# The last stage of a four-layer graph network on Trainium2: thirteen units of four node columns instead of whole-tile steps

## The reference, cut to what matters

```
out  = segment_sum(xl[src] * softmax(logits by dst), dst) + bias     # [N, 4 heads * 16]
mean = out.mean(axis=0); var = out.var(axis=0)                       # over the 6,250 nodes
out  = (out - mean) * rsqrt(var + 1e-5) * gamma + beta
y    = x + gelu(out + x)
result = (y - y.mean(-1)) / sqrt(y.var(-1) + 1e-5)                   # over the 64 features
```

## Time and profile before

| what | us |
|---|---|
| median of 3 runs | 6778.48 (6776.0 to 6781.07) |
| the profiled execution's own time | 6777.28 |
| its span | 6775.5 |
| start of the first gather of the last stage | 6614.07 |
| start of VectorE's work behind the gathers | 6679.11 |
| start of the first store | 6767.56 |

### The profile page before, as it was taken

How to read it: one execution, slowest core, us unless ns; L and a number is a source line. 1 busy time by engine, 2 the same in 40 slices (tenths; PEclk the granted TensorE clock), 3 DMA queues, 4 the chain that set the end, 5 groups by cost and what they waited for, 6 DMA issues and landing times. The chain is left out here.

```text
span 6775.5 us, 58450 instructions
## 1 busy us (share of the span) xinstructions
PE 3900.6 (58%) x12498; PEld 2265.4 (33%) x12498; DVE 3850.9 (57%) x4586; ACT 1823.0 (27%) x3467; POOL 3542.2 (52%) x3649
## 2 busy tenths in 40 slices
PE   3556544675444444444444435777778787777770
PEld 2344432454222222222222223333344344433340
DVE  9988844632333333333333343777787778777774
ACT  1233322342111111111111111333333333333330
POOL 5430032215666666666666656665666556565542
PEclk7666667765776676666676655666666656666665
DMA  5545577502343334333343312333333333333320
GB/s 157 166 155 165 163 164 197 181 8 59 95 102 100 102 99 103 98 102 98 101 103 98 100 40 58 81 84 75 82 86 84 80 80 86 80 81 78 81 69 22
DMA packets 1365705, 671.25 MB, mean 99 GB/s; under 512 B 1042970, under 2 KB 1246324, under 8 KB 1364706
## 3 DMA queue, kind: packets, MB, share of 16 engines
q1 hardware_dynamic: 1090118, 338.26, 21.0%
q0 software_dynamic: 116096, 120.71, 9.5%
q10 hardware_dynamic: 159390, 211.24, 8.9%
HBM read 344.19 MB, written 325.64 MB: 99 GB/s over the span
## 5 line engine op out<-in xcount | busy, mean ns | idle before, releaser
L1565 POOL DMA_INDIRECT got<-tabg,ix x1568 | 1479.0, 943 | 960.3 <-issue 426.0
L1373 POOL DMA_INDIRECT got<-tabg,ix x1568 | 1479.0, 943 | 830.8 <-issue 441.9
L1393 PE MATMUL p_inter<-hid,W 128*128 128x512 f32 x392 | 381.1, 1073 | 1251.9 <-DVE run L1479 983.9
L1471 DVE TENSOR_TENSOR_SCAN own<-mk,own,p_first 128x512 f32<-128x512 bf16 x195 | 248.8, 1276 | 1419.3 <-remote 806.0
L175 PEld LDWEIGHTS p_out<-ident,run 128*128 128x128 f32 (+1 forms) x3136 | 580.8, 219 | 577.7 <-issue 572.1
L175 PE MATMUL p_out<-ident,run 128*128 128x128 f32 (+1 forms) x3136 | 684.2, 372 | 64.5 <-issue 57.0
L490 DVE TENSOR_TENSOR_SCAN run<-p_mk,run,feat 128x512 f32<-128x512 f32 x390 | 477.2, 1265 | 243.2 <-ACT feat L583 84.1
L1393 PEld LDWEIGHTS p_inter<-hid,W 128*128 128x128 f32 x392 | 93.6, 297 | 1295.9 <-issue 1163.3
L1728 DVE TENSOR_TENSOR p_pre<-own,p_pre 128x512 f32<-128x512 f32 x196 | 136.0, 694 | 561.0 <-issue 313.5
L1617 PE MATMUL p_logit<-act_in,AT 128*128 128x512 f32 x392 | 288.7, 826 | 284.9 <-DVE act_in L1734 157.2
L558 PE MATMUL p_mk<-mk,sel 2*128 2x512 bf16 x392 | 166.5, 517 | 450.8 <-DVE run L490 367.3
(11 more groups left out here) (309 smaller groups left out, 7414.7 us busy)
## 6 DMA issues: line engine op xcount, KB each, us to landing
t<-rows ACTq DMA_DIRECT2D x195, 512.0 KB
first<-start SPq DMA_DIRECT2D x780, 128.0 KB
t<-rows ACTq DMA_DIRECT2D x195, 288.0 KB
got<-tabg,ix POOLq DMA_INDIRECT x3136
start<-zeros SPq DMA_DIRECT2D x100, 500.0 KB
ea<-in_ea_dram SPq DMA_DIRECT2D x390, 128.0 KB
mk<-marks SPq DMA_DIRECT2D x780, 64.0 KB
start<-zeros SPq DMA_DIRECT2D x195, 256.0 KB
```

Source lines behind the costliest of these rows:

```text
L1373: nc.gpsimd.indirect_dma_start(got[s][0:g.p, cc, h, :], None, tabg, bass.IndirectOffsetOnAxis(ap=ix[0:g.p, g.n, h, cc:cc + 1], axis=0)).th ...
L1393: nc.tensor.matmul(p_inter[s][:, 0:g.w], W2[:, :], hid[s][:, 0:g.w], start=True, stop=True).then_inc(mixed, 1)
L1471: nc.vector.tensor_tensor_scan(own[s][:, 0:g.w], mk[m][:, 0:g.w], p_first[s][:, 0:g.w], prime[:, 0:1] if g.zero else own[1 - s][:, W - 1:W ...
L1565: nc.gpsimd.indirect_dma_start(got[s][0:g.p, cc, h, :], None, tabg, bass.IndirectOffsetOnAxis(ap=ix[0:g.p, g.n, h, cc:cc + 1], axis=0)).th ...
```

## The change

`finish_4` becomes one block, and `norm` goes. Everything but the clearing, two small preparations and `X + BE` runs by the 13 units of `UNITS`:

- Each unit has its own semaphore for its four gathers. VectorE makes the differences of a unit (`shift`), ScalarE the exponentials (both in one instruction), VectorE the messages (`attend`, one unit behind).
- The sums over nodes are 49 accumulating matmuls each, one for each node column, with `ones` as weights, or `some` (ones only on the full partitions) from column 27 on. For the variance ScalarE squares a unit and TensorE sums it.
- Scale, gelu, residual sum and the last norm's mean and squares run by units in one loop; the last root is still one for all nodes.
- The final scaling goes by units, and SyncE stores each unit behind it. `out_rows` yields the 127 full partitions as one transfer, and in units that reach below column 27 a second one for the last partition: 13 + 7 = 20 transfers.

```diff
@@ -816,42 +816,6 @@
-def norm(nc, sb, sem, ahead, t, o, behind):
...
+def out_rows(out, a, k):
+    yield slice(0, FULLP), k, out[0:FULLP * NJ, :].rearrange("(p j) f -> p j f", j=NJ)[:, a:a + k, :]
+    last = min(LASTJ - a, k)
+    if last > 0:
+        yield slice(FULLP, FULLP + 1), last, out[FULLP * NJ + a:FULLP * NJ + a + last, :].rearrange("(p j) f -> p j f", p=1)
...
             def _(sp):
...
+                stores = 0
+                for u, (a, k) in enumerate(UNITS):
+                    sp.wait_ge(done, u + 1)
+                    for part_, j, rows_out in out_rows(out, a, k):
+                        sp.dma_start(rows_out, out_y[part_, a:a + j, :]).then_inc(written, 16)
+                        stores += 1
+                sp.wait_ge(written, 16 * stores)
             @block.gpsimd
             def _(pool):
                 pool.wait_ge(cleared, 1)
-                gather_rows(pool, nc, rows, T3, t3, info["last"], rows_in)
+                for u, (a, k) in enumerate(UNITS):
+                    for j in range(a, a + k):
+                        nc.gpsimd.indirect_dma_start(rows[:, j, :], None, t3, bass.IndirectOffsetOnAxis(ap=info["last"][:, j:j + 1], axis=0),
+                                                     bounds_check=E - 1, oob_is_err=False).then_inc(rows_in[u], 16)
...
+                def shift(u):
+                    a, k = UNITS[u]
+                    dve.wait_ge(rows_in[u], 16 * k)
+                    wait_from(dve, raised, u - 1)
+                    wait_from(dve, shifted, 2 * u)
+                    link(nc.vector.tensor_tensor(mx[:, 0:k, :], theirs[:, a:a + k, :], rows[:, a:a + k, D + HEADS:T3], ALU.max))
+                    nc.vector.tensor_tensor(dif[u % 2][:, 0:k, 0, :], rows[:, a:a + k, D + HEADS:T3], mx[:, 0:k, :], ALU.subtract).then_inc(shifted, 1)
+                    nc.vector.tensor_tensor(dif[u % 2][:, 0:k, 1, :], theirs[:, a:a + k, :], mx[:, 0:k, :], ALU.subtract).then_inc(shifted, 1)
+                def attend(u):
+                    a, k = UNITS[u]
+                    f, q = fac[u % 2], part[u % 2]
+                    dve.wait_ge(raised, u + 1)
+                    mark(nc.vector.tensor_tensor(q[:, 0:k, 0, :], rows[:, a:a + k, D:D + HEADS], f[:, 0:k, 0, :], ALU.mult))
+                    link(nc.vector.tensor_tensor(q[:, 0:k, 1, :], f[:, 0:k, 1, :], heads(carry[:, D:D + HEADS], k), ALU.mult))
+                    link(nc.vector.scalar_tensor_tensor(out=denom[:, 0:k, :], in0=q[:, 0:k, 0, :], scalar=1e-16, in1=q[:, 0:k, 1, :], op0=ALU.add, op1=ALU.add))
+                    link(nc.vector.reciprocal(rden[:, 0:k, :], denom[:, 0:k, :]))
+                    mark(nc.vector.tensor_tensor(q[:, 0:k, 0, :], f[:, 0:k, 0, :], rden[:, 0:k, :], ALU.mult))
+                    link(nc.vector.tensor_tensor(q[:, 0:k, 1, :], f[:, 0:k, 1, :], rden[:, 0:k, :], ALU.mult))
+                    mark(nc.vector.tensor_tensor(split(msg[:, 0, 0:k, :]), split(rows[:, a:a + k, 0:D]), channels(q[:, 0:k, 0, :], k), ALU.mult))
+                    link(nc.vector.tensor_tensor(split(msg[:, 1, 0:k, :]), split(each(carry[:, 0:D], k)), channels(q[:, 0:k, 1, :], k), ALU.mult))
+                    link(nc.vector.tensor_tensor(msg[:, 0, 0:k, :], msg[:, 0, 0:k, :], msg[:, 1, 0:k, :], ALU.add))
+                    nc.vector.tensor_tensor(Y[:, a:a + k, :], msg[:, 0, 0:k, :], each(BI, k), ALU.add).then_inc(ys, 1)
+                def centre(u):
+                    a, k = UNITS[u]
+                    nc.vector.tensor_tensor(Y[:, a:a + k, :], Y[:, a:a + k, :], each(mean, k), ALU.subtract).then_inc(centred, 1)
+                def scale(u):
+                    a, k = UNITS[u]
+                    link(nc.vector.tensor_tensor(Y[:, a:a + k, :], Y[:, a:a + k, :], each(rg, k), ALU.mult))
+                    nc.vector.tensor_tensor(Y[:, a:a + k, :], Y[:, a:a + k, :], XB[:, a:a + k, :], ALU.add).then_inc(zs, 1)
+                def centre_2(u):
+                    a, k = UNITS[u]
+                    dve.wait_ge(gelus, u + 1)
+                    link(nc.vector.tensor_tensor(out_y[:, a:a + k, :], Y[:, a:a + k, :], X[:, a:a + k, :], ALU.add))
+                    link(nc.vector.tensor_reduce(s_sum[:, a:a + k], out_y[:, a:a + k, :], AX.X, ALU.add))
+                    link(nc.vector.tensor_scalar(s_mean[:, a:a + k], s_sum[:, a:a + k], 1.0 / D, None, ALU.mult))
+                    nc.vector.tensor_tensor(out_y[:, a:a + k, :], out_y[:, a:a + k, :], bn(s_mean[:, a:a + k], k), ALU.subtract).then_inc(zc, 1)
+                def spread_2(u):
+                    a, k = UNITS[u]
+                    dve.wait_ge(z2, u + 1)
+                    nc.vector.tensor_reduce(s_var[:, a:a + k], sq[u % 2][:, 0:k, :], AX.X, ALU.add).then_inc(v2, 1)
...
+                link(nc.vector.tensor_copy(some[:, :], valid[:, LASTJ:LASTJ + 1].to_broadcast((P, P))))
+                mark(nc.vector.tensor_scalar(away[:, :], info["span"][:, :], -1.0, -NEG, ALU.add, ALU.mult))
...
+                nc.vector.tensor_tensor(XB[:, :, :], X[:, :, :], per_feature(BE), ALU.add).then_inc(ready, 1)
+                for u in range(NU + 1):
+                    if u < NU:
+                        shift(u)
+                    if u:
+                        attend(u - 1)
+                dve.wait_ge(total, NU)
+                link(nc.vector.tensor_scalar(mean[:, :], p_sum[:, :], 1.0 / N, None, ALU.mult))
+                for u in range(NU):
+                    centre(u)
+                dve.wait_ge(ready, 1)
+                dve.wait_ge(centred, NU)
+                link(nc.vector.tensor_tensor(rg[:, :], rs[:, :], GA[:, :], ALU.mult))
+                for t in range(NU + 4):
+                    if t < NU:
+                        scale(t)
+                    if 0 <= t - 2 < NU:
+                        centre_2(t - 2)
+                    if 0 <= t - 4 < NU:
+                        spread_2(t - 4)
+                dve.wait_ge(root, 1)
+                dve.wait_ge(zc, NU)
+                link(nc.vector.reciprocal(s_rs[:, :], s_sd[:, :]))
+                for a, k in UNITS:
+                    nc.vector.tensor_tensor(out_y[:, a:a + k, :], out_y[:, a:a + k, :], bn(s_rs[:, a:a + k], k), ALU.mult).then_inc(done, 1)
...
+                def nodes(j):
+                    return some if j >= LASTJ else ones
+                pe.wait_ge(chain, 3)
+                for u, (a, k) in enumerate(UNITS):
+                    pe.wait_ge(ys, u + 1)
+                    for j in range(a, a + k):
+                        mm = nc.tensor.matmul(p_sum[:, :], nodes(j)[:, :], Y[:, j, :], start=j == 0, stop=j == NJ - 1)
+                    mm.then_inc(total, 1)
+                for u, (a, k) in enumerate(UNITS):
+                    pe.wait_ge(squared, u + 1)
+                    for j in range(a, a + k):
+                        mm = nc.tensor.matmul(p_var[:, :], nodes(j)[:, :], sq[u % 2][:, j - a, :], start=j == 0, stop=j == NJ - 1)
+                    mm.then_inc(spread, 1)
             def _(act):
+                for u, (a, k) in enumerate(UNITS):
+                    act.wait_ge(shifted, 2 * u + 2)
+                    wait_from(act, ys, u - 1)
+                    nc.scalar.activation(fac[u % 2][:, 0:k, :, :], dif[u % 2][:, 0:k, :, :], ACT.Exp).then_inc(raised, 1)
+                for u, (a, k) in enumerate(UNITS):
+                    act.wait_ge(centred, u + 1)
+                    wait_from(act, spread, u - 1)
+                    nc.scalar.activation(sq[u % 2][:, 0:k, :], Y[:, a:a + k, :], ACT.Square).then_inc(squared, 1)
+                act.wait_ge(spread, NU)
+                nc.scalar.activation(sd[:, :], p_var[:, :], ACT.Sqrt, scale=1.0 / N, bias=eps[:, 0:1]).then_inc(rooted, 1)
+                for t in range(NU + 3):
+                    if t < NU:
+                        a, k = UNITS[t]
+                        act.wait_ge(zs, t + 1)
+                        nc.scalar.activation(Y[:, a:a + k, :], Y[:, a:a + k, :], ACT.Gelu).then_inc(gelus, 1)
+                    if 0 <= t - 3 < NU:
+                        u, (a, k) = t - 3, UNITS[t - 3]
+                        act.wait_ge(zc, u + 1)
+                        wait_from(act, v2, u - 1)
+                        nc.scalar.activation(sq[u % 2][:, 0:k, :], out_y[:, a:a + k, :], ACT.Square, scale=0.125).then_inc(z2, 1)
+                act.wait_ge(v2, NU)
+                nc.scalar.activation(s_sd[:, :], s_var[:, :], ACT.Sqrt, bias=eps[:, 0:1]).then_inc(root, 1)
...
-        norm(nc, sb, sem, [], Z, Y, [])
...
```

More of the change, by code:

```diff
@@ L1763, in finish_4 @@
         carry = sb(c, "carry", [P, T3])
-        Y, Z = sb(c, "Y", [P, NJ, D]), sb(c, "Z", [P, NJ, D])
+        Y, XB, out_y = sb(c, "Y", [P, NJ, D]), sb(c, "XB", [P, NJ, D]), sb(c, "out_y", [P, NJ, D])
         BI, GA, BE = (sb(c, n, [P, D]) for n in ("BI", "GA", "BE"))
-        inv = sb(c, "inv", [P, NJ])
-        theirs, mx, dif, fac, scaled, denom, rden = (sb(c, n, [P, NJ, HEADS]) for n in ("theirs", "mx", "dif", "fac", "scaled", "denom", "rden"))
```

(35 more changed lines are left out.)

93 lines of the change are left out of this document (5 added, 88 removed).

## The result

The changed kernel takes 6864.07 us in the median (6823.18 to 6881.47, 4 runs), the kernel before 6779.77 in the same session (6776.0 to 6792.22): a ratio of 1.0108, 95% interval 1.0078 to 1.0138. Slower, as forecast (the interval lies clear of 1), but 39 us above the forecast of 6825 and outside its range of 6803 to 6847. That is a coincidence, which a table of the stages brings out. Each number is the distance between two instructions of the timeline: the first memset of the last stage, its first gather, the mean, the reciprocals `rs` and `s_rs`, the end of the span.

A forecast was written before the change was run, and what follows sets the result against it. It took the last stage as bound by GpSimd's gathers (65 us), then VectorE (88), then stores and barrier (9). −25.8 + 5.0 + 1.1 + 0.6 + 66.3 = +47.2 on 6777.28 led to 6825, range 6803 to 6847.

The forecast's parts named there:

- Messages by units, beside the gathers: Last stage's message loop: 3.0 us a unit hides behind 5.2 for its four gathers, so centring starts 25.8 us earlier.
- the rival of slower gathers: Last stage's gathers: VectorE's load slows them by up to 12 us, giving 6837; chance 0.03.
- My own sign: VectorE's last reciprocal, forecast near 6744: if later than 6750, the steps before the stores were mispriced.
- Variance, +5.0: Centring to reciprocal of the root: 49 TensorE matmuls 0.43 us apart make it 22.5 us instead of 17.46, 5.0 lost.
- The rival of a rising clock: Variance: TensorE at full clock, so 49 matmuls take 13.5 us instead of 21.1, giving 6817; chance 0.08.
- Scale, gelu, last norm, +1.1 and +0.6: Loop after the variance: 32.7 us against 31.6, 1.1 lost; last root waits for its table load, 0.6 lost.
- Stores, +66.3: Final stores of 127 partitions queue on one engine: 78.6 us from reciprocal to end instead of 12.3, 66.3 lost.
- The other end of my range: Store stream on one engine at 26 GB/s, 62 us, giving 6812; packet price well off to either side, chance 0.12.
- the divisor rule: Stores: a transfer uses as many engines as the largest divisor of its partitions up to 16, so 127 get one.
- The closing packets: Final stores: small packets that close a transfer on each engine, forecast as 20 instead of 32.
- The sum: Whole change: −25.8 + 5.0 + 1.1 + 0.6 + 66.3 = +47.2 us on the profiled execution's 6777.28.

The follow-up runs named there:

- the large units: Messages of the last stage over four units of 12, 12, 12 and 13 columns instead of 13 units; in the kernel with all repairs, ratio 0.9968 and 0.9969.
- the repaired ones: The changed kernel with stores cut at 112 in three groups, 256-column matmuls for node sums, sum of x and beta behind centring: ratio 0.9958 and 0.9953.

## Why the prediction was wrong

**The failed step is "Messages by units, beside the gathers": centring "25.8 us earlier", "hidden" behind GpSimd.** It gained 3.2 us in the first session, 22.6 less than forecast. The sum put the lateness of hand-offs beside the gathers at nothing. The instructions were sized right: 3.05 us a unit against 3.0 (the loop that waits for all rows). Two things failed. The larger one, some 19 us, is that on that chip hand-offs beside a long run of gathers come 0.4 to 4.5 us late (up to 5.2 in the later traces with lateness), and a unit has seven in a row on VectorE, and one to ScalarE and back. On chip 4, without lateness, the same kernel gains 22.0. Where the lateness comes from stays open. I looked for a slowdown of the gathers by VectorE, and not for one of VectorE by the gathers. My evidence that "VectorE runs beside many of those scatters" came from the earlier trace rows, the durations of GpSimd's instructions; the waits of the other engines in the same chains, shown above, were in the same trace. The smaller one, 3.3 us, is the second gather beside the sum of x and beta: the rival of slower gathers was right in kind, for one gather only, and with a 3.42 us instruction as its cause.

My own sign came true: `s_rs` ended at 6751.35, later than 6750, though the stage had begun 15.5 us early.

**Variance, +5.0:** measured +5.0, paced by TensorE at half clock as said. The rival of a rising clock did not come with 64 columns; it came with 256.

**Scale, gelu, last norm, +1.1 and +0.6:** measured +1.9 together. The table load stands ahead of the last root as said.

**Stores, +66.3:** mechanism right, shown by 54 us on taking it out and on putting it in; size 8.5 us too large. The stream ran at a flat 24 GB/s where I took 22.1 from a transfer that had all 16 engines at work; 1.60 MB at 24 is 67 us, not 75, and 4 were left for lead and tail. The other end of my range, 26 GB/s from the fastest slice, was as near in rate and nearer in time (62 us). By the divisor rule ("DMA: Bandwidth & Descriptors", section "Why a DMA increments its semaphore by 16 and not by 1", of the Trainium skill) 127, 124 and 112 partitions give 1, 4 and 16 engines, and the traces agree: 6.8% and 21.2% of 16 engines, and 54 us between the first and the last. The closing packets are 20, as forecast: the queue shows 1678 packets from 6750 to 6822, of which 1658 are data by my count (12 × 127 + 127 + 7).

**The sum:** +47.2 forecast, +61.5 measured in the first session (22.6 from the messages, less 8.5 from the stores, 0.2 from the loop), +42.8 on chip 4 (3.8 from the messages, less 8.4, the rest alike). There the ratio is 1.0063 (1.0043 to 1.0083); +47.2 on that chip's 6099.4 would be 1.0077, inside that interval. Between the stage's +61.5 and the medians' +84 lie 23 us. They were traced nowhere; I take it that they arose in stages that the change leaves alone, since the two sets have four runs each, of which one spans 58 us, and since the difference of medians was 60 us, the stage's 59, when the changed kernel ran eight times against 27 runs of the one before. The stage's miss of 14 us alone would have left the time inside my range, at 6839; with the 23 it fell outside. That the profiled execution lay 1.7 us from the forecast was luck. My range allowed for nothing of that kind; the 5 us between runs of before in the listed times were no guide to it.

## What to carry to other kernels

Before cutting a store by columns, look at its partitions: 127 ran on one engine at 24 GB/s and 124 on four, and a few wide pieces of 112 with small ones beside them cost less than any of these. Before hiding a chain of short dependent steps beside a run of gathers, find chains in the trace that already run beside one and read the idle time ahead of their instructions, not the instructions' durations: where they stand until the gathers end, the overlap brings less than half of what it does elsewhere (14.8 us on chip 9 against 32 between chips 0 and 4). And compare stages before totals, for a total that fits can be two errors.

## What the runs showed of the hardware

- Sessions, each on its own chip, differ in how soon signals arrive. On the three with late ones the kernel before took 6764 to 6855 us, on the three without 6097 to 6111 (medians, or one execution on chips 13 and 0). The stages between differ too: from the memset that opens layer 2's edges to the second node chain it is 2337 us (first session) and 1979 (chip 4), from there to the last stage 2653 and 2508. In the view of waits (total, count, longest) the longest wait of one weight load that the profile can't explain falls from 18.3 us (first session) to 3.7 (chip 4):

```profile
PEld p_inter L1393 <- issue: 1163.3, 177, 18.3
```

```profile
PEld p_inter L1393 <- issue: 545.2, 171, 3.7
```

That the same lateness makes all of these 650 us was not shown. Nor was its cause found: fewer gathers under way do not change it. Two rivals are untested: something else that ran on the machine in those sessions, and the recording of events itself, since it is in the late stretches that raises go unrecorded and every execution here was recorded. Whether it goes by the hand-off or by the work stays open too, since all three runs of the large units met chips without it.
- A whole-tile VectorE instruction of 3.42 us holds up GpSimd's issue of a gather (3.90 instead of 1.00 us), once, at the start: the issue begins 0.4 us behind the instruction and ends 0.9 us behind its end. It reads two tiles in SBUF, and the gather reads its indices there. The Trainium skill ("SBUF — State Buffer", section "SBUF: two separate sides") says that VectorE and GpSimd hold one pair of ports in turns, each for a whole instruction, a two-input VectorE instruction against a GpSimd one that reads SBUF among them; this trace agrees, and beside the short VectorE instructions the rest of the gathers lose 0.3 us in all, too little to count.
- One DMA engine alone moved 24 GB/s with packets of 1 KB and 25 with packets of 12.5 KB.
- TensorE's granted clock rose from 0.50 to 1.00 within the variance when its matmuls were wide, in the kernel with that edit alone (11.8 us to rs) and in the repaired ones (11.3 to 12.2), and stayed at 0.50 in the same place of the changed kernel (22.7). TensorE was busy nearly all the time in both (20.45 of 20.5 us at 0.50; 3.00 of 3.00 before the rise).
